# Kept column tiles of four chunks of product three, multiplied ahead between the last chunks of product two

## The reference

```python
x = ln(x + adj @ (scale[:, None] * (adj @ (x @ weight))) + bias)           # products one and two
x = ln(x + relu((inv_deg[:, None] * A_prime @ x) @ W.T + b))                # product three, A_prime = a*adj + (1-a)*I
z = leaky_relu(lap_mul(adj, x) @ W1 + b1)                                   # product four
S = exp(-dist(z, z) / 2), all but the 4 nearest of each row set to 0
x = ln(x + lap_mul(S + adj, x) @ W2 + b2)                                   # product five
x = ln(x + relu(concat([x, adj @ x]) @ W.T + b))                            # product six
```

## Time and profile before

| | |
|---|---|
| time, median of 3 runs | 1466.86 us (1465.03 to 1467.11) |
| span of the profiled execution, first to last instruction | 1463.7 us |
| PE busy | 1393.7 us (95%) |
| DVE, ACT, POOL busy | 836.0, 451.0, 246.9 us |
| moved to and from HBM | 403.26 MB, mean 276 GB/s |
| pass 1 (product two) on PE | 372 to 488 us of the span |
| pass 2 (product three) on PE | 491 to 671 us |

### The profile page before, as it was taken

The page is one execution under the profiler, slowest core; times in us unless marked ns, Lnnn a source line. Parts: engine busy times, 40 slices in busy tenths (PEclk is TensorE's granted clock), DMA queues, the critical chain, the costliest instruction groups (busy, mean ns, idle before and its releaser), DMA issues.

```text
span 1463.7 us, 20350 instructions
## 1 busy us (share of the span) xinstructions
PE 1393.7 (95%) x7300; PEld 737.9 (50%) x7300; DVE 836.0 (57%) x1311; ACT 451.0 (31%) x979; POOL 246.9 (17%) x358
## 2 busy tenths in 40 slices
PE   6999999999999799999999987999999889999997
PEld 4776676666444354444544532444444344444454
DVE  6877766665224423323322269999999356555044
ACT  4776665665100000000000045666666200000011
POOL 2111110111100100000000000111111277774000
PEclk9999999999999999999999999999999989999999
DMA  9999998897998979788778520004443799999962
GB/s 311 400 383 389 365 331 300 325 318 266 359 382 331 379 308 346 306 316 328 298 292 310 227 72 1 15 17 137 134 130 115 242 370 401 380 386 394 352 234 71
DMA packets 112814, 403.26 MB, mean 276 GB/s; under 512 B 10368, under 2 KB 28384, under 8 KB 91232
## 3 DMA queue, kind: packets, MB, share of 16 engines
q1 hardware_dynamic: 72672, 314.33, 57.8%
q0 software_dynamic: 20576, 77.07, 14.0%
q10 hardware_dynamic: 19488, 10.80, 2.4%
HBM read 337.67 MB, written 64.49 MB: 275 GB/s over the span
## 4 chain that ended last, share of the span: by engine, by line
PE 70%; DVE 10%; DMA 10%; issue 7%; ACT 2%; POOL 0%; ACTq 0%; SPq 0%; DVEq 0%; POOLq 0%
PE acc L1137 10%; PE acc L1138 9%; PE acc L1139 9%; PE pt L1201 4%; DMA at_scratch<-region 3%; PE pt L1277 3%; PE pt L1278 3%; PE pt L1279 3%; DVE hT L1021 3%; PE pt L1137 3%; PE pt L1139 3%; PE pt L1138 3%; DMA region<-in_adj 3%; PE acc L1186 2%; PE acc L1182 2%
## 5 line engine op out<-in xcount | busy, mean ns | idle before, releaser
L1137 PE MATMUL acc<-region,yop 128*128 128x512 f16 x681 | 259.6, 381 | 16.6 <-DMA region<-at_scratch 16.6
L1201 PE MATMUL pt<-ident,region 128*128 128x128 f32 x1024 | 243.1, 277 | 18.8 <-DMA region<-in_adj 9.6
L1138 PE MATMUL acc<-region,yop 128*128 128x512 f16 x681 | 259.5, 381 | 0.0
L1139 PE MATMUL acc<-region,yop 128*128 128x512 f16 x681 | 259.5, 381 | 0.0
L969 DVE SCALAR_TENSOR_TENSOR region<-pt,region 128x512 f16<-128x512 f32 x200 | 135.3, 686 | 76.9 <-ACT region L631 76.4
L1201 PEld LDWEIGHTS pt<-ident,region 128*128 128x128 f32 x1024 | 145.9, 143 | 61.2 <-issue 16.1
L677 ACT ACTIVATE region<-pt 128x512 f32<-128x512 f32 x256 | 132.8, 602 | 109.4 <-PE pt L1284 95.8
L631 ACT ACTIVATE region<-pt 128x512 f16<-128x512 f32 x200 | 117.8, 596 | 108.6 <-PE pt L1201 94.0
L1021 DVE MAX8 hT<-region 128x8 f32<-128x4096 f32 x32 | 141.2, 4411 | 2.4 <-ACT region L677 2.4
L1137 PEld LDWEIGHTS acc<-region,yop 128*128 128x128 f16 x681 | 66.7, 98 | 98.7 <-issue 14.6
L598 ACT ACTIVATE std<-mv,eps_ln 128x4 f32<-128x4 f32 x32 | 9.5, 297 | 334.5 <-DVE mv L803 334.5
(11 more groups left out here) (235 smaller groups left out, 2157.8 us busy)
## 6 DMA issues: line engine op xcount, KB each, us to landing
region<-at_scratch SPq DMA_DIRECT2D x166, 1280.0 KB, 7.8
region<-in_adj SPq DMA_DIRECT2D x64, 1024.0 KB, 8.9
at_scratch<-region POOLq DMA_DIRECT2D x40, 768.0 KB, 7.0
at_scratch<-region POOLq DMA_DIRECT2D x40, 512.0 KB, 7.6
region<-at_scratch SPq DMA_DIRECT2D x76, 256.0 KB, 2.7
x_scratch<-xout ACTq DMA_DIRECT2D x16, 256.0 KB, 12.3
gath_all<-x_scratch POOLq DMA_DIRECT2D x12, 256.0 KB, 4.1
xin<-at_scratch SPq DMA_DIRECT2D x12, 256.0 KB, 2.8
```

The lines of the kernel that those rows point to most:

```text
L1137: nc.tensor.matmul(into, y[:, 0, kt, :], high, start=(kt == first_tile), stop=False)
L1138: nc.tensor.matmul(into, y[:, 0, kt, :], low, start=False, stop=False)
L1139: return nc.tensor.matmul(into, y[:, 1, kt, :], high, start=False, stop=(kt == last_tile))
L1201: ins = nc.tensor.transpose(pt[kt % 4][:, t * P:(t + 1) * P], nat[u % 4][:, t, (kt % TPC) * P:(kt % TPC + 1) * P], ident[:, :])
```

## The change

PE multiplies the seven kept tiles of chunks 2 to 5 of pass 2 (`AHEAD2`) already in pass 1, each into a `pt` bank of its own: those of chunk 2 behind chunk 5 of pass 1, those of chunk 3 behind chunk 6, those of chunks 4 and 5 behind chunk 7 (`AHEAD2_BEHIND`, new function `kept_ahead`). The projections of pass 1's chunks 5, 6 and 7 move: each now stands right behind the kept tiles that follow its own chunk (that of chunk 7 was inside the first chunk of pass 2). In pass 2, chunks 2 to 5 start at tile 7 and go on in their `pt` bank, and DVE reads the sum from there (`pass_acc`). Their turn and projection come after the same number of tiles from the chunk's start. PE and DVE now run pass 2 with all chunks unrolled. No transfer is added, removed or reordered in SP's or POOL's programs.

```diff
+AHEAD2 = [2, 3, 4, 5]
+AHEAD2_BEHIND = {5: [2], 6: [3], 7: [4, 5]}
...
+        def pass_acc(p, c, par):
+            return pt[AHEAD2.index(c)] if p == 2 and c in AHEAD2 else acc[par]
...
-                    nc.vector.scalar_tensor_tensor(hT[:, :], acc[par][:, :], alpha_acc[:, 0:1], xT[:, :], ALU.mult,
-                                                   ALU.add).then_inc(hT_ready, 1)
+                    nc.vector.scalar_tensor_tensor(hT[:, :], pass_acc(2, c, par)[:, :], alpha_acc[:, 0:1], xT[:, :],
+                                                   ALU.mult, ALU.add).then_inc(hT_ready, 1)
...
-            epilogues(2)
+            for c in range(NCH):
+                counted(2, c, lambda: epilogue(2, c, c % 2, c // 2))
+            close(2)
...
-                    pe.wait_ge(hT_ready, n - 2)
-                    for kt in range(KT):
-                        if p == 1 and kt < early_tiles(c):
-                            continue
-                        start = early_tiles(c) if p == 1 else 0
+                    ahead = p == 2 and c in AHEAD2
+                    start = early_tiles(c) if p == 1 else KEPT if ahead else 0
+                    if not ahead:
+                        pe.wait_ge(hT_ready, n - 2)
+                    for kt in range(start, KT):
...
-                        last = products(p, acc[par][:, :], kt, hi, lo, start)
+                        last = products(p, pass_acc(p, c, par)[:, :], kt, hi, lo, 0 if ahead else start)
...
-                            if p == 1 and kt == KT - 1 and kt - start < PROJECT_AT[p]:
-                                pe_project(pe, p, c - 1)
-                            pe_epilogue_at(pe, kt - start, p, c - 1, 1 - par, m - (1 - par))
+                            if not (p == 1 and c - 1 in AHEAD2_BEHIND):
+                                pe_epilogue_at(pe, kt - start, p, c - 1, 1 - par, m - (1 - par))
...
-                        else:
+                        elif p != 2:
                             pe_epilogue_at(pe, kt, before, NCH - 1, 1, PAIRS - 1)
+
+                def kept_ahead(c):
+                    for kt in range(KEPT):
+                        if kt % TPC == 0:
+                            pe.wait_ge(yop_ready, nth(YOP, 1, kt // TPC))
+                        products(2, pass_acc(2, c, None)[:, :], kt, kept[:, c, kt, 0, :], kept[:, c, kt, 1, :])
+
                 if p == 1:
+                    for c in range(NCH):
+                        chunk(c, c % 2, c // 2)
+                        for c2 in AHEAD2_BEHIND.get(c, []):
+                            kept_ahead(c2)
+                        if c in AHEAD2_BEHIND:
+                            pe_project(pe, 1, c)
+                elif p == 2:
                     for c in range(NCH):
                         chunk(c, c % 2, c // 2)
```

## The result

The median went from 1466.98 us (1465.03 to 1467.61, 4 runs) to 1453.34 us (1452.15 to 1455.45, 4 runs). The ratio of the runs is 0.9897, with a 95% interval of 0.9877 to 0.9918: faster, by 12.0 to 18.0 us. The forecast was 12.1 us less, 1454.8, with a range from 1452.8 to 1459.5. The 12.1 us lie at the small end of the interval. The sign and the mechanism were right; the size was too small by 1.5 us by the medians and by 3.0 by the ratio, and the range left no room for that.

The account below looks back on a forecast made before the run. PE bounds the kernel, busy for 95% of the span, but is starved in pass 1's last short chunks. Gaps and slow clock there, 12.1 us, off 1466.86 give 1454.8 us, range 1452.8 to 1459.5.

Parts of the forecast that it names:

- The gaps: End of pass 1 into pass 2: four PE gaps, together 9.03 us, plus 3.07 us of slow clock behind two.
- the prices: PE's cost per piece of work: 0.648 us a tile, 4.53 us for seven kept tiles, 0.49 for a projection.
- the walk-through: New order from 474.46 us: no PE wait, pass 2 at 501.83, its sixth tile 6.0 us later, 12.1 us gained.
- Chunks 2 to 5 at no loss: Pass 2: each falls from 22.05 to 17.52 us and transfers keep up; loss taken as nothing, bounds nothing and 4.6.
- The first rival: Transfers bind in chunks 2 to 5 of pass 2: 1458.3 us, or 1463.4 without reserve; chance 0.08.
- the slower one: Memory gives only 315 GB/s in chunks 2 to 5 of pass 2: 2.6 us slower, 1469.5; chance 0.03.
- The reserve: Lag of loads in pass 2's chunks 2 to 5 before PE notices: 5.1 us at the least.
- The epilogues: DVE's epilogues at pass 1's end let projections 6 and 7 start without waiting, 2.5 and 4.5 us early.
- the rivals of the epilogues and of no change: Epilogues set the tail's pace, 1457 to 1461, chance 0.05; same gaps return behind the moved tiles, 1466.9, chance 0.02.
- the Sum: Whole kernel: 12.1 us off the span of 1463.7 gives 1451.6; median 3.2 above the span; 1454.8 us.
- unrolling is taken at nothing either way: Pass 2 unrolled on PE and DVE was claimed to cost and gain nothing.
- The spread of 1 us: Whole kernel: the runs' own spread, about 1 us either way, in the forecast's reach of 1453.3 to 1456.5.

Follow-up runs that it names:

- extra_3: The changed kernel with 256 KB more loaded, unused, behind three of the five units of each of pass 2's chunks 3 to 6: 1454.11 us.
- extra_5: The changed kernel with 256 KB more loaded, unused, behind all five units of each of pass 2's chunks 3 to 6: 1456.40 us.
- two_chunks: The changed kernel with only the kept tiles of chunks 2 and 3 made ahead, none behind chunk 7: 1459.51 us, ratio 0.9939.
- fill_twice: The changed kernel, but pass 2 multiplies the kept tiles of chunks 2 to 5 again and ignores the sums made ahead: 1470.18 us, ratio 1.0011.

## Why the prediction was right in kind and short in size

- **The gaps, the prices and the walk-through** held for the trace that they were read from: 12.1 us forecast, 12.3 measured between the two first traces, with 27.21 us for 27.37. The rest is that a projection costs 0.44 at full clock and I had taken the 0.49 of a row behind a gap.
- **Chunks 2 to 5 at no loss** held: 17.52 us each with PE busy throughout. The first rival and the slower one fell with these chunks and with `extra_3`, at 411 GB/s. The reserve was sized by landings of 7.9 us at the most; they rose to 10.8, so that by the prediction's own sum 2.2 us of the 5.1 were left in the changed kernel, and PE noticed nothing. By `extra_5` there was more.
- **The epilogues** held, with 2.9 and 4.2 us to spare; no gap came back behind the moved tiles, so that the rivals of the epilogues and of no change fell; `two_chunks` shows the price of losing the second cover, 6.4 us.
- **The step that failed is the Sum** (and the range laid around it): one trace was taken for the kernel, so that the term for the gaps was too small, and the unrolling was put at nothing. First, "12.1 us off the span": that trace had the shortest tail of the kernel's four. The changed kernel has no waits there, and a tail of 184.13 in all three traces, so what it wins is what the kernel before loses in the execution at hand: 12.3 us by the first trace, 12.6, 12.8 and 14.8 by the others, 13.1 on average. Second, "unrolling is taken at nothing either way" was wrong by 1.0 us in the store stretch, and at a place that nobody would look for it: 750 us later, where a load of instructions no longer falls into a store (though the first trace of the changed kernel gave that microsecond back one store later). A further 0.35 us lie outside the span. Together some 14.4 us, of 13.6 by the first medians and 15.3 by the later, larger set. What may be left, up to a microsecond, stays open: from the end of pass 2 to the first projection of product six it took 722.3 to 722.9 us in the kernel before and 722.0 to 722.1 in the changed one, but 721.7 to 724.0 in the other kernels, so it is not to be put down to the change. The same sum would make `fill_twice` 3.6 us slower than before; measured are 0 to 3.2, which stays open too.
- **The spread of 1 us** came from three runs. 29 runs of the same kernel span 9.3 us, and the end of chunk 5 alone lies between 474.5 and 477.1 us in its four traces. The range should have reached some 3 us below the forecast; above it, it reached 4.7.

## What to carry to other kernels

Filling a wait with work that is due later anyway pays its full length as long as the later stage is bound by the engine that was filled; walk it through instruction by instruction, and look at what each cover has to spare: here one chunk's tiles behind each short chunk look better than two behind the last, by 1.8 us in one trace. A stretch with waits in it is also where executions differ, so one trace of it is a sample. What took the waits away took that stretch's scatter with them, though not the kernel's: the ten runs of `fill_twice`, without these waits, still span 5.7 us. And a change of an engine's program length moves later loads of its instructions, which here went with a microsecond won far away.

## What was unexpected of the hardware

- A load of 16 KB of instructions for PE that starts 5.6 to 5.7 us behind the issue of a store of 256 KB goes with a store that lands about 1 us later (five traces: 8.2 to 8.4 us for 7.0 to 7.4, store stretch 15.0 to 15.2 us for 14.1 to 14.3). In `fill_twice`, 6.4 us behind the issue, it cost nothing.
- Loads from HBM together with the passes' small stores ran at 411 to 413 GB/s over 72 us (`extra_3`, `extra_5`).
